# Another order of the four engines' work in the repeated body of the two stacks, with the groups of value products side by side

## The reference

```python
x = x + 0.5 * _L2_ffn_ref(_layernorm(x, axis=-1), ...)      # stack 1
x = x + _L2_attn_ref(_layernorm(x, axis=-1), ...)
x = x + 0.5 * _L2_ffn_ref(_layernorm(x, axis=-1), ...)      # stack 2

def _L2_ffn_ref(x, ...):
    for i in range(DEPTH):                                   # DEPTH = 6
        x = attn_layer(shift_tokens(x), Wqkv[i], q_scale[i], k_scale[i], Wo[i]) + x
        x = ffn_layer(shift_tokens(x), ln_g[i], ln_b[i], W1[i], b1[i], W2[i], b2[i]) + x

def attn_layer(x, Wqkv, qs, ksc, Wo):                        # 16 heads of 64, windows of 32
    q, k, v = split(x @ Wqkv)
    q, k = l2norm(q) * qs, l2norm(k) * ksc                   # then rotated by position and scaled
    out = local_attention(q, k, v)                           # each window sees itself and the one before
    return out @ Wo

def ffn_layer(x, g, bln, W1, b1, W2, b2):
    a, gate = split(layernorm(x) * g + bln) @ W1 + b1
    return a * gelu(gate) @ W2 + b2
```

## Time and profile before

| | |
|---|---|
| median of 3 runs | 5368.52 us (5355.53 to 5376.36) |
| the profiled execution | 5368.35 us, span 5366.6 us |
| PE busy | 4978.9 us (93%) |
| DVE, ACT, POOL busy | 3814.0 (71%), 3438.1 (64%), 2867.6 us (53%) |
| mean granted TensorE clock | 0.951 of full speed; full speed (1.00) in the steady part of both stacks |
| stack 1, from its first projection to its last result | 1040.2 to 2763.4 us |
| stack 2, the same | 3026.3 to 4763.6 us |

### The profile page before, as it was taken

One profiled execution on the slowest core, in us unless ns is written; L12 is line 12 of the kernel. 1 busy time (PEld: TensorE's weight loads), 2 busy tenths in 40 slices (PEclk: granted clock), 3 DMA queues, 4 the chain that ended last, 5 costly groups with the idle time before them and its releaser, 6 DMA issues. The chain is left out here.

```text
span 5366.6 us, 141783 instructions
## 1 busy us (share of the span) xinstructions
PE 4978.9 (93%) x49044; PEld 3454.0 (64%) x49044; DVE 3814.0 (71%) x7030; ACT 3438.1 (64%) x5879; POOL 2867.6 (53%) x3451
## 2 busy tenths in 40 slices
PE   8988977499999999999969699999999999989889
PEld 5655655267777777777745367777777777756556
DVE  2243236488888888888856488888888888845545
ACT  3333323278888888888845378888888888832642
POOL 0010005378788778778720288777787787700200
PEclk9989988599999999999979799999999999989899
DMA  1000000011111111112100111111111111110000
GB/s 44 1 5 34 1 1 9 29 45 55 51 50 51 55 51 49 51 51 55 43 15 1 40 39 55 51 51 49 55 51 55 46 55 51 39 34 7 1 25 9
DMA packets 110454, 195.51 MB, mean 36 GB/s; under 512 B 21409, under 2 KB 28849, under 8 KB 110257
## 3 DMA queue, kind: packets, MB, share of 16 engines
q1 hardware_dynamic: 110256, 192.82, 12.8%
HBM read 53.29 MB, written 1.05 MB: 10 GB/s over the span
## 5 line engine op out<-in xcount | busy, mean ns | idle before, releaser
L2674 POOL TENSOR_TENSOR stage_qk<-stage_halves 128x1024 f32<-128x1024 f32 x384 | 906.0, 2359 | 53.3 <-DVE stage_halves L2790 45.8
L2710 POOL TENSOR_TENSOR stage_qk<-stage_qk,stage_rnorm 128x1024 f32<-128x1024 f32 x384 | 730.9, 1903 | 30.5 <-issue 0.3
L2703 POOL TENSOR_TENSOR stage_probs<-stage_probs,stage_rsum 128x768 f32<-128x768 f32 x384 | 565.3, 1472 | 222.1 <-DVE stage_rsum L2819 209.6
L2787 DVE TENSOR_TENSOR stage_halves<-stage_wide,stage_tables 128x1024 f32<-128x1024 f32 x384 | 468.2, 1219 | 227.6 <-ACT stage_square L2493 187.4
L2493 ACT ACTIVATE stage_square<-stage_wide 128x1024 f32<-128x1024 f32 x384 | 394.0, 1026 | 191.9 <-PE stage_wide L2259 191.5
L2325 PE MATMUL stage_pv<-stage_probsT,stage_v_win 96*64 96x64 f32 x12288 | 488.1, 227 | 2.7 <-ACT stage_ctxT L2546 1.6
L2790 DVE TENSOR_TENSOR stage_halves<-stage_wide,stage_tables 128x512 f32<-128x512 f32 x768 | 490.5, 680 | 0.0
L2325 PEld LDWEIGHTS stage_pv<-stage_probsT,stage_v_win 96*64 96x64 f32 x12288 | 408.4, 137 | 122.7 <-issue 98.5
L2799 DVE TENSOR_REDUCE stage_norm<-stage_square 128x16 f32<-128x1024 f32 x384 | 464.7, 1210 | 30.8 <-issue 30.7
L2276 PE MATMUL stage_turn<-ident,stage_qk 128*128 128x128 f32 x3072 | 478.9, 279 | 4.9 <-ACT stage_qkT L2513 4.7
L2311 PEld LDWEIGHTS stage_flip<-ident,stage_probs 128*96 128x96 f32 x3072 | 355.6, 126 | 194.3 <-issue 130.0
(11 more groups left out here) (299 smaller groups left out, 9877.6 us busy)
## 6 DMA issues: line engine op xcount, KB each, us to landing
stage_v_win<-stage_v SPq DMA_DIRECT2D x384, 192.0 KB, 2.5
stage_v_win<-stage_v SPq DMA_DIRECT2D x384, 128.0 KB, 2.4
stage_v_win<-stage_v SPq DMA_DIRECT2D x192, 64.0 KB, 2.2
stage_wq<-in_T_wq SPq DMA_DIRECT2D x12, 512.0 KB, 4.1
stage_wk<-in_T_wk SPq DMA_DIRECT2D x12, 512.0 KB, 4.7
stage_wv<-in_T_wv SPq DMA_DIRECT2D x12, 512.0 KB, 3.5
stage_wo<-in_T_wo SPq DMA_DIRECT2D x12, 512.0 KB, 3.5
stage_w_up<-in_L_w_up SPq DMA_DIRECT2D x8, 512.0 KB, 6.6
```

Source lines behind the costliest of these rows:

```text
L2674: nc.gpsimd.tensor_tensor(qk[:, n, :], halves[:, n % 2, 0, :], halves[:, n % 2, 1, :], ALU.add)\
L2703: nc.gpsimd.tensor_tensor(probs[:, m % 2], probs[:, m % 2], rsum[:, m % 2].to_broadcast([P, 2, 2 * HALVES, REACH]), ALU.mult)\
L2710: nc.gpsimd.tensor_tensor(heads, heads, rnorm[:, n, :].rearrange("p (h o) -> p h o", o=1).to_broadcast([P, LH, LD]), ALU.mult).then_inc(at ...
L2787: nc.vector.tensor_tensor(out[:, 0], heads, cos.to_broadcast([P, LH, LD]), ALU.mult)
```

## The change

All four `body` functions (PE, ACT, POOL, DVE) get another order. The set of parts is the same: every call in the old bodies is in the new ones, once. No operation, no wait inside a part, no buffer and no transfer is changed, and SP's program is not touched. The letters change too: before, a body spans the steps e, s, u, w, and now g, e, s, u.

The diff of PE's body, cut to the places where the value products stand:

```diff
             def body(s):
                 g, e, u, w = s - 2, s - 1, s + 1, s + 2
                 if runs(s):
-                    weigh(s, 0)
+                    project(s, 4)
+                if runs(g):
+                    output(g)
...
-                if runs(s):
-                    score(s, 3)
-                if runs(s):
-                    weigh(s, 1)
...
+                if runs(e):
+                    weigh(e, 0)
+                if runs(e):
+                    weigh(e, 1)
...
+                if runs(e):
+                    weigh(e, 4)
+                if runs(e):
+                    weigh(e, 5)
...
+                if runs(e):
+                    weigh(e, 6)
+                if runs(e):
+                    weigh(e, 7)
+                if runs(g):
+                    down(g)
```

More of the change, by code:

```diff
@@ L2414, in body @@
[L2414 to L2446, removed]
@@ L2565, in body @@
                 g, e, u, w = s - 2, s - 1, s + 1, s + 2
+                if runs(e):
+                    exponential(e, 1)
+                if runs(s):
+                    copy_qkT(s, 0)
+                if runs(s):
+                    copy_v(s, 0)
+                if runs(e):
+                    copy_probsT(e, 0)
+                if runs(e):
+                    lay_band(e, 3)
+                if runs(s):
+                    copy_v(s, 1)
                 if runs(u):
-                    copy_v(u, 0)
+                    shifted_z(u)
@@ L2724, in body @@
+                if runs(s):
+                    refine(s, 3)
+                if runs(s):
+                    scale(s, 3)
+                if runs(e):
+                    normal_probs(e, 2)
                 if runs(u):
-                    clamp(u, 3)
+                    clamp(u, 0)
                 if runs(u):
-                    scale(u, 2)
+                    sum_turns(u, 0)
+                if runs(u):
+                    refine(u, 0)
+                if runs(e):
+                    normal_probs(e, 3)
@@ L2868, in body @@
                 g, e, u, w = s - 2, s - 1, s + 1, s + 2
+                if runs(s):
+                    norms(s, 3)
+                if runs(e):
+                    shift(e, 2)
+                if runs(e):
+                    sum_probs(e, 1)
+                if runs(g):
+                    add_output(g)
+                if runs(g):
+                    statistics(g)
+                if runs(e):
+                    shift(e, 3)
+                if runs(g):
+                    normalize(g)
@@ new lines, in body @@
+                if runs(e):
+                    sum_probs(e, 3)
+                if runs(u):
+                    rotate(u, 1)
+                if runs(u):
+                    norms(u, 1)
+                if runs(g):
+                    gated(g, 0)
+                if runs(s):
+                    shift(s, 0)
+                if runs(g):
+                    gated(g, 1)
+                if runs(u):
+                    rotate(u, 2)
+                if runs(u):
+                    norms(u, 2)
@@ L2916, in _ @@
+                if runs(g):
+                    gated(g, 2)
+                if runs(s):
+                    shift(s, 1)
+                if runs(u):
+                    rotate(u, 3)
+                if runs(g):
+                    add_ffn(g)
+                if runs(s):
+                    sum_probs(s, 0)
             for s in range(-2, 2):
```

334 lines of the change are left out of this document (148 added, 186 removed).

## The result

The changed kernel takes 5330.26 us (median of 6 runs, 5324.07 to 5336.15), the one before 5370.16 us (6 runs). The ratio is 0.993 with a 95% interval of 0.9916 to 0.9945: faster by 0.7%. The profiled executions are 5368.35 and 5326.59 us.

What follows compares the result with a forecast made beforehand. PE's matmuls set the period. Steady bodies gain 7.5 and 16.7 us, fill loses 8.4, drain gains 2.7, P2 loses 8.8: -9.7 from 5368.35 gives 5359 us. Own range 5346 to 5372; full range 5342 to 5412.

Steps and rivals of the forecast that it cites:

- the wait at P1: Projection P1 waits for rotation 0 in the old order; 0.22 us a body in stack 1, 0.40 in stack 2, would go.
- PE's own cost: PE's work per body without waits, summed over small-matmul entries, value-product ends and first full groups: 1.73 before, 1.77 now, +0.04.
- 6 x 0.10, now 5 x 0.10: Cost at the end of each run of value products on PE: 0.10 us each, six runs before, five now.
- 0.50, now 0.55: Cost in us per body of first full-array groups behind small matmuls: 0.10 for projections, up2 and down, 0.05 for transposes.
- I allow 0.10 us per body: Allowance for P2 being late behind P1's square and rotation, with 0.01 to 0.10 us to spare; bounds 0 and 0.3.
- The drain: End of each stack: last step's S2 and transposes move ahead of the last-but-one output, -1.35 us per stack, -2.7 together.
- The fill: Start of each stack, first projection to first output: +4.4 us in stack 1, +4.0 in stack 2, 8.4 lost together.
- the 2.5 us to landing: Value transfers after W7 were said to land at most 2.5 us after all are issued, 5.6 us in all.
- A: Rival: P1's wait turns up whole at P2; period 34.5 to 34.6 us, 5375 us in all; chance 0.15.
- D: Rival: everything fits, P2 too, and the fill is no longer than now; 5341 us; chance 0.08.
- B: Rival: the loop's branch at the seam shows, with P4's load late; 0.3 us a body, 5385 us; chance 0.10.
- C: Rival: DVE becomes the bound, its waits (2.9 us counted) exceeding 4.1; period 35.0, 5413 us; chance 0.20.
- Values: `copy_v` 0 may wait for transfers until 2.9 us into the body; 0.8 us of waiting hidden by output's 3.5.

## Why the prediction was wrong, step by step

The mechanism was right: PE sets the period, the wait at P1 and the late output of stack 2 vanish, both stacks get the same period, P2 is not late, and neither the seam nor DVE becomes a bound. Three terms of the sum were wrong in size, and all three erred to the same side.

**PE's own cost, "+0.04".** Measured: the period without a wait was 34.22 and is 34.11, so -0.11. Two parts of the sum failed. "6 x 0.10, now 5 x 0.10" for the ends of value products took the pair as 1.12, from W2 and W3; that pair has a late load, while W6 and W7 of the same body take 1.08, and so do all three of after (means over 31 bodies: 1.115, 1.083 and 1.083). With 0.615 for a single one, the eight products of before sum to 4 x 0.615 + 1.115 + 1.083 = 4.66 and those of after to 2 x 0.615 + 3 x 1.083 = 4.48: -0.18, where I had -0.10. The first groups behind, "0.50, now 0.55", are 0.50 and 0.50 by the rows: up2 loses 0.07 and two of the transposes behind scores 0.04. With the entry (+0.09) this makes -0.09, and the output, 0.01 shorter, brings it near the -0.11. 0.16 us off in 88 bodies is 14 us.

**"I allow 0.10 us per body" at P2.** Measured 0: P2's load stands ahead, 5.80 behind P1, and the kernel with P2 moved up shows that 5.65 is enough. I had taken the chain of P0 to P1, 5.71 and 5.80, for that of P1 to P2 and added 0.10 for the load to be ahead. 88 bodies, 9 us.

**The drain, "-2.7".** Measured -13.0, and -10.5 and -10.3 in the two other executions of the same kernel. I had counted S2 and its transposes as the groups that move. By the counts of the windows it is S2 and the last step's P4, which now stands ahead of the output of two steps before: 2.85 us of the 4.35 in stack 1, twice my 1.35. What I also left out is that PE does not set the pace there: it idles a fifth of the time, and each order has its own sum of waits. The clock over the last output, 1.7 us, was not in the sum either. Both windows of stack 1 ahead of it show 1.00 in both kernels. The order alone does not decide it, since the changed kernel had its last output of stack 2 at 1.00 in one execution and at 0.65 and 0.63 in two others; what does decide it stays open.

The fill, +8.4, came out at +10.4, an error to the other side: +7.2 in stack 1 where I had +4.4, +3.2 in stack 2 where I had +4.0. The first output of stack 1 comes 96.84 us behind the first projection, just above my 94 to 96. PE is busy for 69.9 us of this stretch (521 matmuls, clock 0.81) and was for 63.8 of 89.6 (484, clock 0.83). So 6.1 of the 7.2 us are PE's work, at a clock below the steady body's 1.00, and 1.1 are waits; I had priced it by the steady body.

Two readings of the prediction were also off without moving the sum. The wait at P1 and the output make up 0.18 of the 0.21 between the stacks; the other 0.03 stands at the transposes ahead of the output. And the 2.5 us to landing is a median, not "at most".

Of the rivals, A did not come (P2 has no wait). D came in full for its period and beyond it, though the fill did grow. Two more can be read off. B: the branch lies directly ahead of P4, and tq0 takes 0.49, as it does everywhere behind small matmuls, and P4 1.72, its load 0.11 ahead. The branch costs nothing that the trace shows. The Trainium skill (TensorE: Matmul & The Clock Gate, Engine queue depths) gives PE a queue that would cover it; the trace agrees in that no idle is there. C: DVE idles 34.11 - 30.90 = 3.2 us, and its waits are 0.80 at the statistics, 0.43 and 0.32 ahead of rotations 0 and 1, 0.27 at `gated` 1 and 0.18 at `add_output`, 2.0 in all where I had 2.9. They are not quite the five that I named: `shift` 3 does not wait, and `add_output` and `norms` 3 (0.37) do, both without a releaser in the profile. Values: `copy_v` 0 waits for the transfers by this row of ACT's timeline, and starts 2.46 us behind P4, where I had 2.9 as the latest; P5 stands 5.6 behind P4 and is not touched.

```profile
1993.43 1.02 ACT L2502 ACTIVATE stage_v<-stage_wide 128x1024 f32<-128x1024 f32 x1 [1.58 <-DMA stage_v_win<-stage_v]
```

The chances failed with the sum. I gave the case in which all fits 0.08 and put it at 5341, a number that already contained the 0.04 and the small drain. An error of 0.15 us a body is 0.004 us for each of some 40 groups, less than the second decimal shows; times 88 it is 13 us, more than the whole gain that I forecast. A range should have carried it.

## What to carry to other kernels

Where one engine sets the period and the groups differ in the shape of the array, price each kind of run from all its occurrences, not from one, and multiply by the bodies before deciding what is small. Then lay the order out and ask, for every group that is taken out of a place, what copy or what bank it was covering: pairing alone cost 1.1 us a body here, and it gained only in the order where other work stood in its place. Orders of several engines that are written by hand belong together: with POOL's alone left as it was, a body took 7 us more.

## What the runs showed of the hardware

Small matmuls cost at both edges of a run: 0.09 us to enter, and for the first full-size group behind 0.10 if it is a projection or `down`, 0.07 if it is `up`, 0.04 to 0.06 if it is transposes. Two groups of value products side by side take 1.08 us against 2 x 0.615. Merging two runs gave 0.19 us, undoing a pair cost 0.30. A projection whose first load is not ahead takes 1.82 us, not 1.72. The loop's branch, 0.218 us by its own row, costs nothing that the trace shows even where a projection follows it at once (1.72).
